# A graph layer's kernel: feature products in single-pass float32, in bursts, from one count buffer

## The reference

```python
src_h = h[src] @ W_msg.T + b_msg
msg = src_h + edge_embed[clip(edge_type, 0, 8)]
messages = segment_sum(msg, dst, num_segments=num_nodes)
gi, gh = messages @ W_ih.T + b_ih, h @ W_hh.T + b_hh      # 3 x 128 columns each
r, z = sigmoid(i_r + h_r), sigmoid(i_z + h_z)
n = tanh(i_n + r * h_n)
out = layernorm(x + (1 - z) * n + z * h)
```

## Time and profile before

| | |
|---|---|
| median of three runs | 1468.43 us |
| the profiled execution | 1467.18 us, span 1465.1 us |
| busy: PE, weight loads, DVE, ACT, POOL | 1092.5, 873.6, 837.6, 638.8, 827.4 us |
| granted clock of TensorE, mean | 0.901 |
| moved by DMA | 118.02 MB, mean 81 GB/s |
| chain that ended last | PE 64%, issue 13%, ACT 10%, an unknown queue 9%, DVE 2% |

### The profile page before, as it was taken

The page is one execution under the profiler, slowest core; times in us unless marked ns, Lnnn a source line. Parts: engine busy times, 40 slices in busy tenths (PEclk is TensorE's granted clock), DMA queues, the critical chain, the costliest instruction groups (busy, mean ns, idle before and its releaser), DMA issues.

```text
span 1465.1 us, 33091 instructions
## 1 busy us (share of the span) xinstructions
PE 1092.5 (75%) x13301; PEld 873.6 (60%) x13301; DVE 837.6 (57%) x2652; ACT 638.8 (44%) x1217; POOL 827.4 (56%) x811
## 2 busy tenths in 40 slices
PE   5456787776777877787778788787888887887764
PEld 1134666565565665666666666566667776676642
DVE  7425465556656654665556556565566665565434
ACT  4542133453444434544444445444445443544413
POOL 7636666555556655565556555555556554555440
PEclk9765689899999988999999999899999999999987
DMA  8682122222222222222222222222222222222221
GB/s 215 181 274 87 45 61 72 66 68 72 79 64 71 72 66 63 74 74 73 69 68 78 71 66 71 71 70 73 66 75 68 79 64 69 66 77 65 71 75 30
DMA packets 95897, 118.02 MB, mean 81 GB/s; under 512 B 20091, under 2 KB 81399, under 8 KB 95736
## 3 DMA queue, kind: packets, MB, share of 16 engines
q0 software_dynamic: 36800, 76.33, 19.8%
q1 hardware_dynamic: 57080, 37.80, 8.8%
q10 hardware_dynamic: 1856, 1.68, 0.5%
HBM read 99.74 MB, written 16.00 MB: 79 GB/s over the span
## 4 chain that ended last, share of the span: by engine, by line
PE 64%; issue 13%; ACT 10%; another core or an unknown queue 9%; DVE 2%; DMA 1%; SPq 1%; DVEq 0%; ACTq 0%
PE psf L998 27%; PE psb L983 17%; ACT mem L1102 7%; PE psg L965 4%; PE pAB L940 4%; PE pAB L926 4%; PE psg L961 2%; ACT L1089 2%; PE psg L970 2%; PE pAB L943 1%; DMA arena<-in_x 1%; PE pAB L871 1%; PE psf L1003 1%; SPq L423 1%
## 5 line engine op out<-in xcount | busy, mean ns | idle before, releaser
L516 POOL DMA_INDIRECT xg<-x_split,idx x680 | 703.0, 1034 | 518.2 <-PE psg L965 354.6
L998 PE MATMUL psf<-mem 128*128 128x128 f16 x7644 | 645.8, 230 | 93.0 <-issue 58.6
L1102 ACT CAST mem<-psb 128x432 f16<-128x432 f32 x832 | 398.6, 524 | 651.6 <-PE psb L983 464.0
L998 PEld LDWEIGHTS psf<-mem 128*128 128x128 bf16 x7644 | 540.8, 104 | 155.9 <-issue 92.0
L771 DVE TENSOR_TENSOR ohk<-iota,prm 128x392 bf16<-128x392 f16 (+3 forms) x842 | 314.5, 415 | 371.4 <-PE psb L983 274.2
L983 PE MATMUL psb<-ohk,ohl 128*128 128x108 bf16 (+3 forms) x1801 | 416.1, 271 | 148.1 <-ACT mem L1102 79.8
L983 PEld LDWEIGHTS psb<-ohk,ohl 128*128 128x128 bf16 x1801 | 169.3, 104 | 214.8 <-issue 110.1
L779 DVE TENSOR_TENSOR ohl<-iota,prm 128x512 bf16<-128x512 f16 x421 | 176.6, 419 | 0.0
L802 DVE TENSOR_TENSOR mem<-mem,psg 128x112 f32 (+10 forms) x192 | 56.8, 296 | 156.3 <-PE psg L970 82.8
L965 PE MATMUL psg<-ohs,xg 128*128 128x56 bf16 (+9 forms) x2040 | 112.1, 202 | 37.8 <-issue 37.3
L516 POOL DMA_INDIRECT xg<-in_x,idx x88 | 90.4, 1027 | 61.7 <-PE psg L961 35.0
(11 more groups left out here) (123 smaller groups left out, 734.4 us busy)
## 6 DMA issues: line engine op xcount, KB each, us to landing
xg<-x_split,idx POOLq DMA_INDIRECT x680
x_split<-mem SPq DMA_DIRECT2D x24, 384.0 KB
xb<-in_xT SPq DMA_DIRECT2D x49, 128.0 KB
arena<-in_xN SPq DMA_DIRECT2D x49, 128.0 KB
arena<-in_x SPq DMA_DIRECT2D x24, 256.0 KB
out<-spill SPq DMA_DIRECT2D x19, 128.0 KB
out<-arena SPq DMA_DIRECT2D x16, 128.0 KB
out<-arena SPq DMA_DIRECT2D x128, 8.0 KB
```

The source lines that it names most:

```text
L516: pool.indirect_dma_start(out=xg[:, p % RING, :] if split else xg32(p % RING), out_offset=None, in_=x_d if split else x, in_offset=bass.In ...
L998: ins = pe.matmul(psf[:, q % 2, 0:FB], xs[0:kk, h, c, :], Bb[q % 2][0:kk, HT + h, :], start=(h == 0 and c == 0), stop=(h == HI - 1 and c = ...
L1102: act.copy(Bb[q % 2][:, :, n:n + MOST], psb[:, bank % NB, 0:MOST * HC].rearrange("p (d h) -> p h d", h=HC)).then_inc(S["s_eb"], 1)
```

## The change

- The features are split in two parts, both single-pass float32, which sum to x exactly; the second subtraction and the third copy go. `xs` holds two parts of 4 bytes.
- A feature product takes the counts as the loaded weights and both parts as 256 moving columns: 98 products for a block instead of 294. The result lies turned and in two parts; ACT copies it (`("S", q)`), and PE adds the parts and turns them back with the identity (`("T", q)`).
- The counts are float32 and there is one count buffer. The casts are items (`("K", bank)`), and the first of a block waits for the feature products of the block before.
- The items of a block come in two pieces: a burst (the 49 feature parts with the slots that fit in the three banks, and a step of the final stages after every fourth part) and the rest of the slots with the sparse groups, each with two steps.
- All sparse groups gather raw rows from x and multiply in float32. `x_split` and SP's writes of it go; the ring holds 128 float32 values a row.
- The slots' keys go through a scratch in memory: ACT stores each turned set (`prm_d`) and loads them back in columns of 128 slots into a `prm` with room for two. Two turns are behind all units, two in the first two groups. The flag's sum is behind the first two turns.
- Small tiles share one tile, and the weights `wms` and `wih` lie in the arena.

The diff, cut to its core:

```diff
-PRE = UNITS + 2
+PRE = UNITS + 1
-SWITCH = 22
-STEPS = (3, 4)
+STEPS = 4
+BURST = 13.0
+SPREADOUT = 18.0
+EVERY = 4
+BETWEEN = 2
-TURN_AT = (15, 18)
-SUM_AT = 21
-XS = 3 * HI * H // 2
+CH = 2
+XS = 2 * HI * H
+READY_TURNS = 2
...
+def cycles():
+    out = []
+    for q in range(NQ + 1):
+        own = [i for i, d in enumerate(DS) if PLACE[d[0]] // FB == q]
+        limit = q * (FB // MOST) + NB
+        first = [i for i in own if all(b < limit for b, _, _, _ in pieces(i))] if q else []
+
+        def casts(i):
+            return [("K", b) for b, _, _, _ in pieces(i) if BANK_LAST[b] == i]
+
+        burst, rest = [], []
         if q:
+            mixed = sorted([((k + 0.5) / PARTS, 0, ("F", q - 1, k)) for k in range(PARTS)] +
+                           [((k + 0.5) / len(first), 1, ("B", i)) for k, i in enumerate(first)])
+            burst = [u for _, _, u in mixed] + [u for i in first for u in casts(i)]
+        for i in own[len(first):]:
+            rest.append([("B", i)] + casts(i))
+        sums = [[("S", q - 1)], [("T", q - 1)], [("C", q - 1)]] if q else []
+        for k, u in zip((2, 6, 12), sums):
+            rest.insert(k + 1, u) if own else rest.append(u)
+        out.append((burst, rest))
+    return out
...
+    plan = cycles()
+    spans = [(BURST if burst else 0.0) + SPREADOUT for burst, rest in plan[:-1]]
...
+    spent, total = 0.0, sum(spans)
+    for q, (burst, rest) in enumerate(plan):
+        for k, u in enumerate(burst):
+            items.append(u)
+            if u[0] == "F" and u[2] % EVERY == 2:
+                items += advance(g, 1)
+        if q < len(spans):
+            spent += spans[q]
+            n = LEAD + round((GROUPS - REST - LEAD) * spent / total) - g
+        else:
+            n = 3
+        at = sorted((len(rest) * (2 * k + 1)) // (2 * n) for k in range(n)) if n else []
+        due = []
+        for k, chunk in enumerate(rest + [[]]):
+            while at and at[0] <= k:
+                at.pop(0)
+                items += due
+                items += group(g)
+                items += advance(g, BETWEEN)
+                lb.append(float(low))
+                due = closing(g)
+                g += 1
+            items += chunk
...
-        xs = mem[:, 0:XS].bitcast(BF16).rearrange("p (h c f) -> p h c f", c=3, h=HI)
-        Bb = [b.bitcast(F16).rearrange("p (h d) -> p h d", h=HC) for b in bw]
+        with nc.sbuf_tensor("xs", [P, HI, 2, H], F32R) as xs, nc.sbuf_tensor("sides", [P, 2 * (R + W)], F32), \
+                nc.sbuf_tensor("Bb", [P, HC, FB], F32R) as Bb:
+            pass
...
-                pool.wait_ge(S["s_xw"], 16 * (UNITS + 1))
-                for p in range(SWITCH * G, NG):
-                    gather(p, True)
+                for p in range(RING, NG):
+                    gather(p)
...
-            for t in range(PRE):
+            for t in range(UNITS):
                 split(t)
-                if t in TURN_AT:
-                    turn(TURN_AT.index(t))
-                if t == SUM_AT:
-                    pe.wait_ge(S["s_bad"], 1)
-                    pe.matmul(psg[0:1, 2 * P:2 * P + J + 2], one[:, :], badc, start=True, stop=True,
-                              skip_group_check=True).then_inc(S["s_sum"], 1)
-            for a in range(len(TURN_AT), len(TURNS)):
+            for a in range(READY_TURNS):
                 turn(a)
+            pe.wait_ge(S["s_bad"], 1)
...
-                            if g < SWITCH:
-                                ins = pe.matmul(g2[:, 0, 0:w], xg32(p % RING), oh[:, j, :], start=(j == 0),
-                                                stop=(j == G - 1), skip_group_check=True)
-                            else:
-                                for c in range(3):
...
+                            pe.matmul(g2[:, 0, 0:w], xg32(p % RING), oh[:, j, :], start=(j == 0),
+                                      stop=(j == G - 1), skip_group_check=True).then_inc(S["s_used"], 1)
...
-                            for c in range(3):
-                                ins = pe.matmul(psf[:, q % 2, 0:FB], xs[0:kk, h, c, :], Bb[q % 2][0:kk, HT + h, :],
...
+                            pe.matmul(psf[:, q % 2, 0:2 * H], Bb[0:kk, HT + h, :], xs[0:kk, h, :, :].rearrange("p c f -> p (c f)"),
+                                      start=(h == 0), stop=(h == HI - 1), skip_group_check=True)
...
+                    elif it[0] == "T":
+                        q = it[1]
+                        pe.wait_ge(S["s_sc"], q + 1)
+                        for c in range(2):
+                            ins = pe.matmul(psf[:, q % 2, 2 * FB:3 * FB], part[:, c, :], ident[:, :], start=False, stop=(c == 1),
+                                            skip_group_check=True)
+                        ins.then_inc(S["s_tt"], 1)
...
             def turned(a):
                 j0, j1 = TURNS[a]
-                cols, n = slice(j0 * P, j1 * P), (j1 - j0) * P
+                k = j1 - j0
+                if a:
+                    act.wait_ge(S["s_pd"], 16 * a)
                 for c in range(3):
                     i = 3 * a + c
                     act.wait_ge(S["s_tm"], i + 1)
...
+                act.wait_ge(S["s_te"], 3 * (a + 1))
+                act.dma_start(prm_d[j0:j1].rearrange("j p n -> p j n"),
+                              stage[:, 0:k, :, :, :].rearrange("p j c n t -> p j (c n t)")).then_inc(S["s_pd"], 16)
+
+            def load_keys(j):
+                act.wait_ge(S["s_pd"], 16 * (j // 4 + 1))
+                if j >= CH:
+                    act.wait_ge(S["s_ok"], (j - CH + 1) * P // OB)
+                act.dma_start(prm[:, j % CH, :, :, :].rearrange("p c n t -> p (c n t)"), prm_d[j]).then_inc(s_pk[j % CH], 16)
...
+                    elif it[0] == "K":
+                        bank = it[1]
+                        q, n = bank * MOST // FB, bank * MOST % FB
+                        act.wait_ge(S["s_kd"], BANK_LAST[bank] + 1)
+                        if bank == 0:
+                            act.wait_ge(S["s_pd"], 16 * len(TURNS))
+                        elif n == 0:
+                            act.wait_ge(S["s_fd"], q)
+                        act.copy(Bb[:, :, n:n + MOST], psb[:, bank % NB, 0:MOST * HC].rearrange("p (d h) -> p h d", h=HC)
+                                 ).then_inc(S["s_eb"], 1)
+                    elif it[0] == "S":
+                        q = it[1]
+                        act.wait_ge(S["s_fd"], q + 1)
+                        act.copy(part[:, :, :], psf[:, q % 2, 0:2 * H].rearrange("p (c f) -> p c f", c=2)).then_inc(S["s_sc"], 1)
```

More of the change, by code:

```diff
@@ L198, in step, with group @@
         return out
-    for g in range(GROUPS):
+    def group(g):
         ub.append(float(clear - W))
@@ L203, in schedule @@
         assert top + MARGIN < clear - W
[L204 removed]
+        out = [("G", g)]
+        if READY_TURNS + g < len(TURNS):
+            out.append(("turn", READY_TURNS + g))
         if g == READY:
[L206 to L217 removed]
@@ L229, in schedule @@
+    late = done
+    while g < GROUPS:
+        items += group(g)
+        parts = [advance(g, 1) for _ in range(STEPS)]
+        lb.append(float(low))
+        items += parts[0] + closing(g)
+        for part in parts[1:]:
+            items += part
+        g += 1
     while active or first or main:
@@ L534, in _ @@
                                             ).then_inc(s_rec[k], 16)
-            for p in range(FIRST, SWITCH * G):
-                gather(p, False)
+            for p in range(FIRST, RING):
+                gather(p)
             pool.wait_ge(S["s_fl"], 1)
```

217 lines of the change are left out of this document (85 added, 132 removed).

## The result

The changed kernel takes 1711.9 us (median of 4 runs), the kernel before 1473.6 in the same comparison: ratio 1.160, 95% interval 1.150 to 1.170. The forecast was 1232, in a range of 1110 to 1370. All ratios in this text leave out executions more than 1.5% above the fastest of their kernel, so they can differ a little from the quotient of the medians. The profiled execution has a span of 1708.3 us and a mean granted clock of 0.777.

A forecast was written before the change was run, and what follows sets the result against it. The prediction took PE, an in-order queue losing time to waits on ACT and DVE, as the bound. From a span of 1465.1 us it took 160 for the cycles and 75 for the start, giving 1230, forecast 1232; range 1110 to 1370.

The forecast's parts named there:

- The start and the end: Before and after the steady cycles: first block ending at 147 us instead of 222.3, minus 75; the 58.6 us tail stays.
- Part 1: Dense feature products: 98 single-pass float32 pairs of load and product at 0.11 us replace 294, minus 5.6 us a cycle.
- Rival 4: Feature products: weight load and product do not overlap, a pair costs about 0.21 us, total 1420 to 1530; chance 0.11.
- Part 2: Sparse products on raw float32 rows: plus 0.41 us for 170 groups, 70 us of PE work, about 2.9 a cycle.
- Part 3: One count buffer and bursts: a cycle of 15 + 26 = 41 us instead of 47.4, minus 160 us in 25 cycles.
- the spread stretch: Rest of a cycle after its burst, with remaining count products, casts and sparse groups: 26 us, bounds 21.5 and 32.
- the present 15.5 us of waiting: Old cycle of 47.4 us: 15 to 16 us read as waiting; two thirds of it kept gave the upper bound 32.
- Rival 3: The waiting stays outside the bursts: that stretch 30 to 32 us, cycle 45 to 47, total 1330 to 1380; chance 0.20.
- the signs: What the new trace should show, such as 41 us cycles, products 0.105 to 0.12 us apart, POOL idle about a tenth.
- Rival 2: POOL's gathers bind at 35.2 us a cycle: cycle falls to 36 us, total 1107 up to 1170; chance 0.17.

The follow-up runs named there:

- e13: e12 with gathers for the first 17 rows only (wrong rows afterwards); 1093.2 us, ratio 0.977 to the kernel before.
- e4: Kernel before the change, with all sparse products on raw float32 rows, its order and two count buffers kept; 1439.6 us, ratio 1.010.
- e18: The same edit to the kernel before as e4, run again in another set; 1445.9 us, ratio 1.002.
- e17: Changed kernel with each sparse product a single bf16 product of the raw row's upper 16 bits; 1630.9 us, ratio 1.129 to the kernel before.
- e12: Changed kernel put back in the old order with two count buffers, keeping float32 feature products, raw sparse rows and keys through memory; 1121.2 us, ratio 1.000.
- e1: Changed kernel with gathers for the first 17 rows only (wrong rows afterwards); 1288.7 us, ratio 0.903 to the kernel before.
- e3: Changed kernel with two of a cycle's seven sparse groups moved into the burst; 1477.3 us, ratio 1.034 to the kernel before.
- e9: Changed kernel itself, unedited, run again on a quiet chip; 1293.6 us, ratio 1.153 to the kernel before.
- e7: Kernel before with all sparse products on raw float32 rows and gathers for the first 17 rows only; 1113.5 us, ratio 0.994.
- e5: Changed kernel with later gathers landing in two ring rows that TensorE never reads or waits for; ratio 1.291 to the kernel before, cycle 44.1 us.
- e6: Changed kernel with each gather after the 17th replaced by a direct copy of 128 neighbouring rows; ratio 1.133 to the kernel before, cycle 44.2 us.
- e15: The same edit to the changed kernel as e6, run again; ratio 1.136 to the kernel before, cycle 44.0 us.
- e16: The same edit to the changed kernel as e5, run again; ratio 1.314 to the kernel before, cycle 44.1 us.
- e2: Changed kernel with four extra bf16 products behind each count slot outside the bursts; 1802.6 us, ratio 1.267 to the kernel before.

## Why the prediction was wrong

**The start and the end** were right: first sparse product at 79.7 us (forecast 85, 75 to 100), first block's end 147.7 for 147, tail 60.1 for 58.6. That 147.7 fits so well is partly luck: on a quiet chip the same mark stands at 122.3. From the first sparse product to the first burst (at 129.2, and 102.3 on the quiet chip) it took 49.5 us with steps and 34.1 without, for 42 in my sum, which knew no steps.

**Part 1, the pair of 0.11 us,** was nearly right for bursts. It is 0.12 in a run of its own kind (702.69 to 703.40 for six). But behind a bf16 product the next float32 one comes only 0.20 us after the first: in e13 a unit of 0.36 us is 0.04 from count to feature product and 0.12 back, which leaves 0.20 between the two. That is near the upper end of my range for the pair, 0.21, and it eats all but 0.9 us of the saving wherever the products are mixed with others. The rule of the Trainium skill that I had weighed ("TensorE: Matmul & The Clock Gate", section "The mechanism": a load overlaps running products only where their row groups differ) would make every pair 0.21; a sentence above it in the same section also lets a load run ahead if it goes to the background weight buffer, and then it would not. The runs in bursts do not agree, at 0.12; the pair behind a bf16 product would, at 0.20. Rival 4, which needed 0.20 everywhere, did not happen. The rows the price came from were uneven as well: L943's first product starts at 1033.41, 1.00 us after L940's first and 0.77 before the next L998, not 1.35 and 0.42 as I had divided the 1.77.

**Part 2,** 70 us of TensorE work, costs 0 to 20 us of time (e4, e18). The work is real (e17, which takes out more than part 2 put in, has 138 us less of it), but in the old order it found room: on a quiet chip e12, which has part 2, takes 36.3 us a cycle for 36.0, both near POOL's 35.2.

**Part 3 is the step that failed,** the spread stretch of 26 us, "bounds 21.5 and 32". On a quiet chip it held for the block shown, 26.7 us, DVE busy 21.9 of them, 82%, just as taken (only PE's busy time, 19.9, is above the 14.2 of my sum, and it is not the limit); the average of the 25 is 28.4, with bursts of 16.5 for 15, so a cycle is 44.9 for 41. On the chip of the comparison the same stretch took 44.3. The upper bound was made of "the present 15.5 us of waiting, two thirds of it kept", and that sum is where it broke: of these 15.5 us a cycle 47.4 - 36.0 = 11.4 are not there on a quiet chip. They came with the steps, not with the way of a bank through ACT and DVE, which I took them for, and no order tried here is free of them. The new order met more of them, 60.0 - 44.9 = 15.1 us a cycle. That the gathers bring them is shown (e1: 44.1 on a chip with steps); that it is POOL beginning its gathers again behind a burst, beside a TensorE whose work there is a chain with DVE and ACT, fits e3 and the timeline but was not tried by itself.

**The comparison itself.** Even without steps the forecast has the wrong sign, although the 1293.6 us of e9 lie within its range. Quiet, the change is minus 49 us at the start (122.3 for 171.7), plus 25 x 8.9 = 223 in the cycles, minus 2 at the end: 172, which is the difference of the spans, 1292.7 - 1120.4. Of the 8.9 us the order with one buffer costs about 8.6 (e12 has 36.3, and e9 44.9, and they share the float32 products and casts, the raw rows and the keys by way of memory). On the chip with steps it is minus 75, plus 25 x 12.6 = 315, plus 2: 242 of the 243 us between the spans. So two errors lay on top of each other: the new order was priced about 4 us a cycle too low, and the old one was seen 11.4 us worse than its own work makes it. The forecast of 41 would be a loss against 36.0.

**The rivals.** Rival 3, the waiting stays, had the right place, the spread stretch, but too small a price, 47 us for a cycle, and took the waiting for the kernel's own. None had the waiting grow. Rival 4 alone had the sign, by a mechanism that did not happen. Of the signs, POOL was to be idle a tenth of the time; it waits 615.4 us for TensorE's reads. Rival 2, POOL as the floor, describes the kernel before rather than the changed one: on a quiet chip its cycle is 36.0 us, with POOL's gathers needing 35.2 and TensorE 35.4 to 36.3 without them (e13, e7). Both limits meet there, so faster feature products had next to nothing to win in the old order.

**What stays open:** what in a gather holds TensorE's signals back by multiples of 0.71 us on some chips, and why not on others. e5, e6, e15 and e16 were made to separate issue, landing and indices, and all fell on quiet chips. That it is the chip, and not the hour or something beside the kernel, is likely but not shown: one quiet chip was quiet in two sets, every other chip had one. No version here beats the kernel before; e1, e7 and e13 are below it only by leaving gathers out.

## What to carry to other kernels

Before a change is priced by the waiting that it removes, ask of the waits who ends them. Waits that end by "remote" or "issue", beside a TensorE whose starts or signals are multiples of 0.7 us apart, may belong to the chip, and so may part of the waits for a named producer (464.0 us against 308.3 for the same casts); a run on a second chip tells. Then compare the cycle with the floor of every queue: here 36.0 against POOL's 35.2 said that the old order had next to nothing left to give. And one buffer fewer is a barrier: with the bursts made for it, it split a cycle in two stretches in which different engines stand, and cost 8.6 us on 36, more than faster products brought back (3.3).

## What the runs showed of the hardware

- The same kernel, the one before, takes 1118 to 1122 us on two chips (three sets) and 1439 to 1474 elsewhere. In the slower sets starts or signals of TensorE at times come at multiples of 0.71 us, beside float32 or bf16 products, at a granted clock of 1.0 (436 us in before) as at 0.5 (933 to 942 us in after). Without gathers the waits for "remote" are gone from the steady part (e1).
- A float32 product of 256 columns in one pass costs 0.12 us in a row of its kind (e9) and 0.20 behind the first one that follows a bf16 product (e13).
- Extra TensorE work brought the mean clock from 0.777 to 0.845 and no time (e2: 1802.6 us for 1711.9).
- On a quiet chip POOL's gathers cost a TensorE that waits for none of them nothing (44.1 us a cycle in e5 and e16, as in e1 without gathers), and one that waits for them 0.8 to 0.9 us a cycle (44.9 in e9; 36.3 in e12 for 35.4 in e13).
